# A residual of two gathered products: another way to the first adapter, the first x and the last y

## The reference

```python
def reference(x, itok_B_0_15, itok_B_3_7, L0_cond_weights, L1_cond_weight):
    W = L0_cond_weights[itok_B_0_15]                # (128, 64, 64): one of 16 per sample
    x = x + einsum('bct,bcd->bdt', x, W)            # x is (128, 64, 1024) float32
    w = L1_cond_weight[itok_B_3_7]                  # (128, 1024, 1024): one of 8 adapters
    x = x + einsum('bsi,boi->bso', x, w)
    return x
```

## Time and profile before

| | us |
|---|---|
| median of 3 runs | 836.09 |
| lowest, highest | 834.12, 836.31 |
| the profiled execution | 834.99 |
| its span in the profile | 833.2 |
| TensorE (PE) busy | 808.3 (97%) |
| VectorE (DVE) busy | 449.6 (54%) |
| ScalarE (ACT) busy | 280.6 (34%) |
| GpSimd (POOL) busy | 27.4 (3%) |
| DMA | 90.87 MB, mean 109 GB/s |

### The profile page before, as it was taken

One profiled execution on the slowest core, in us unless ns is written; L12 is line 12 of the kernel. 1 busy time (PEld: TensorE's weight loads), 2 busy tenths in 40 slices (PEclk: granted clock), 3 DMA queues, 4 the chain that ended last, 5 costly groups with the idle time before them and its releaser, 6 DMA issues.

```text
span 833.2 us, 17872 instructions
## 1 busy us (share of the span) xinstructions
PE 808.3 (97%) x3572; PEld 668.5 (80%) x3573; DVE 449.6 (54%) x466; ACT 280.6 (34%) x515; POOL 27.4 (3%) x61
## 2 busy tenths in 40 slices
...
DMA packets 74271, 90.87 MB, mean 109 GB/s; under 512 B 13844, under 2 KB 65044, under 8 KB 74260
## 3 DMA queue, kind: packets, MB, share of 16 engines
...
...
HBM read 57.15 MB, written 33.55 MB: 109 GB/s over the span
## 4 chain that ended last, share of the span: by engine, by line
PE 96%; DMA 1%; DVE 1%; issue 1%; SPq 1%; ACTq 0%; POOL 0%; POOLq 0%; ACT 0%; DVEq 0%
PE z_ps L431 14%; PE first_ps L431 14%; PE z_ps L430 14%; PE first_ps L430 14%; PE z_ps L433 14%; PE first_ps L433 13%; PE y_ps L445 4%; PE y_ps L446 4%; PE y_ps L444 4%; DMA w_nat<-in_L_cond_weight_dram 1%; SPq L343 0%; DMA slot_row<-table_i 0%; DMA ids_i<-in_itok_B_dram 0%; PE first_ps L411 0%; ACTq L192 0%
## 5 line engine op out<-in xcount | busy, mean ns | idle before, releaser
L430 PE MATMUL z_ps<-w_hi,xt_hi 128*128 (+1 forms) x528 | 205.5, 389 | 0.0
L431 PE MATMUL z_ps<-w_lo,xt_hi 128*128 (+1 forms) x528 | 205.4, 389 | 0.0
L430 PE MATMUL first_ps<-w_hi,xt_hi 128*128 x528 | 205.4, 389 | 0.0
L431 PE MATMUL first_ps<-w_lo,xt_hi 128*128 x528 | 205.4, 389 | 0.0
L433 PE MATMUL z_ps<-w_hi,xt_lo 128*128 (+1 forms) x512 | 199.2, 389 | 0.0
L433 PE MATMUL first_ps<-w_hi,xt_lo 128*128 x480 | 186.7, 389 | 0.0
L715 DVE STREAM_TRANSPOSE x_turned<-x_in 128x1024 f32<-128x1024 f32 x67 | 143.6, 2143 | 23.9 <-issue 19.5
L524 ACT ACTIVATE xt_hi<-x_turned 128x1024 fp32r<-128x1024 f32 x67 | 71.1, 1061 | 227.7 <-DVE x_turned L715 227.7
L724 DVE TENSOR_TENSOR xt_lo<-x_turned,xt_hi 128x1024 fp32r<-128x1024 f32 x62 | 76.1, 1228 | 77.8 <-ACT xt_hi L524 77.8
L430 PEld LDWEIGHTS z_ps<-w_hi,xt_hi 128*128 128x128 f32 x528 | 99.2, 188 | 20.9
L430 PEld LDWEIGHTS first_ps<-w_hi,xt_hi 128*128 128x128 f32 x528 | 99.1, 188 | 20.8
...
## 6 DMA issues: line engine op xcount, KB each, us to landing
x_in<-in_x_dram SPq DMA_DIRECT2D x544, 64.0 KB, 2.0
out_dram<-y ACTq DMA_DIRECT2D x128, 256.0 KB, 3.1
w_nat<-in_L_cond_weight_dram SPq DMA_DIRECT2D x128, 128.0 KB
...
x_turned<-in_L_cond_weights_dram SPq DMA_DIRECT2D x2, 256.0 KB, 3.9
ids_i<-in_itok_B_dram SPq DMA_DIRECT2D x2, 0.5 KB, 2.1
```

What stands on the lines that cost most here:

```text
L430: nc.tensor.matmul(to, xt_hi[h][:, t, :], whi, start=(t == 0), stop=False)
L431: mm = nc.tensor.matmul(to, xt_hi[h][:, t, :], wlo, start=False, stop=last and not pair)
```

## The change

The first adapter's number no longer comes from the groups: VectorE multiplies 8, 7, ... 1 by "used" and takes the largest (`first_row`). SP waits for that, loads chunks 0 to 5 at once, then x of slot 0 as plain rows in two transfers, its samples read straight from `table_i`, then chunks 6 and 7. TensorE turns x of slot 0 between chunks 3 and 4, through the same PSUM banks, and ACT and VectorE keep it from there. The table is moved by a DMA of ACT's queue, behind ACT's first chunk; GpSimd does chunks 0 to 3, the table's column, chunks 4 and 5, the group steps (on `is_group`, now made behind the table), chunks 6 and 7. The +1 on W goes from GpSimd to VectorE, between the one-hot matrices and the gathered values; the rest of W is made after the chunks instead of before them.

ACT's loop is now an odd and an even slot, and the last slot stands behind it, where y of the slot before is stored ahead of the second half of z. The last y is summed with the matmul on `z_lo` last, ACT writes its first half and VectorE its second, and SP and ACT store a sample each, in halves. The diff, declarations and unchanged arguments left out:

```diff
+        X0 = "x of slot 0"
+        TURN_ORDER = [0, 1, 2, 3, X0, 4, 5, 6, 7]
+        TURN_OF = {what: i for i, what in enumerate(TURN_ORDER)}
+        FOR_FIRST_HALF = 5
...
+        def store_last(eng, k, pairs_past):
+
+            s = 2 * pairs_past + 1
+            *samples, stores = look(eng, s, SAMPLE_A, SAMPLE_B, STORES)
+            rows = slice(k * C, (k + 1) * C)
+            to = out_rows[bass.ds(samples[k] * C, C), :]
+            with eng.If(stores > k):
+                eng.wait_ge(y_made, 4 * pairs_past + 3)
+                eng.dma_start(to[:, 0:HALF], y[1][rows, 0:HALF]).then_inc(last_stored, 16)
+                eng.wait_ge(last_half_made, 1)
+                eng.dma_start(to[:, HALF:T], y[1][rows, HALF:T]).then_inc(last_stored, 16)
+            with eng.Else():
+                eng.sem_inc(last_stored, 32)
...
+            for c in range(4):
+                add_1_to_first(c)
+            pool.wait_ge(table_moved, 16)
+            nc.gpsimd.tensor_copy(slot_row[:, 1:LOOKED_UP + 1, CHUNKS_BEFORE], slot_row[:, 0:LOOKED_UP, CHUNKS]
+                                  ).then_inc(table_ready, 1)
+
+            for c in range(4, 6):
+                add_1_to_first(c)
             pool.wait_ge(groups_made, 1)
...
-            for c in range(2, CHUNKS_PER_GROUP):
+            for c in range(6, CHUNKS_PER_GROUP):
                 add_1_to_first(c)
...
-            sp.wait_ge(groups_ready, 1)
-            first_ad = sp.value_load(group_row[0:1, 0:1], min_val=0, max_val=NAD - 1)
+            sp.wait_ge(first_known, 1)
+            first_ad = sp.value_load(first_row[0:1, 0:1], min_val=0, max_val=NAD - 1)
 
...
-                    sp.wait_ge(first_turned, NH * (c - OWN_PLACE) + NH)
+                    sp.wait_ge(first_turned, NH * TURN_OF[c - OWN_PLACE] + NH)
                 sp.dma_start(first_nat[c], adapter_rows[bass.ds((first_ad * CHUNKS_PER_GROUP + c) * P, P), :]
                              ).then_inc(first_loaded[c], 16)
 
-            for c in range(2):
+            for c in range(6):
                 load_first(c)
 
             sp.wait_ge(table_made, 1)
-            sp.dma_start(slot_row[:, 1:LOOKED_UP + 1, :], table_i[0:LOOKED_UP]).then_inc(table_moved, 16)
-            for c in range(2, 5):
+            _, first_samples = nc.values_load_multi_w_load_instructions(
+                table_i[0:1, SAMPLE_A:SAMPLE_B + 1], engines=[sp.engine], min_val=0, max_val=B - 1,
+                skip_runtime_bounds_check_because="the table is made on the chip, of clipped indices")
+            for k, sample in enumerate(first_samples):
+                sp.dma_start(x_in[0][k * C:(k + 1) * C, :], x_rows[bass.ds(sample * C, C), :]).then_inc(x0_loaded, 16)
+            for c in range(6, CHUNKS_PER_GROUP):
                 load_first(c)
...
             pairs_past = look_pairs_past(sp)
-            load_x(0, 0)
-            for c in range(5, CHUNKS_PER_GROUP):
-                load_first(c)
             load_x(1, 1)
 
-            sp.wait_ge(first_turned, NH * CHUNKS_PER_GROUP)
+            sp.wait_ge(groups_ready, 1)
+            sp.wait_ge(first_turned, NH * len(TURN_ORDER))
+            sp.sem_inc(x_loaded[0], PER_X)
...
+            store_last(sp, 0, pairs_past)
...
-                sp.wait_ge(y_stored[h], 32 * pairs_past + 32 + STORED_AHEAD)
+                sp.wait_ge(y_stored[h], 32 * pairs_past + (STORED_AHEAD if h else 32 + STORED_AHEAD))
                 sp.sem_inc(all_done, 1)
+            sp.wait_ge(last_stored, 64)
+            sp.sem_inc(all_done, 1)
...
+            def turn_first(i):
+                if TURN_ORDER[i] == X0:
+                    pe.wait_ge(x0_loaded, 32)
+                    nat = x_in[0][:]
+                else:
+                    pe.wait_ge(first_with_1, TURN_ORDER[i] + 1)
+                    nat = first_nat[TURN_ORDER[i]]
...
-                        pe.wait_ge(first_lo_made, NH * (c - TURNS) + n + 1)
+                    if i >= TURNS:
+                        pe.wait_ge(first_lo_made, NH * (i - TURNS) + n + 1)
...
             def first_half(pair):
-                pe.wait_ge(xt_lo_made, 1)
-                pe.wait_ge(first_lo_made, NH * TPB)
+                pe.wait_ge(first_lo_made, NH * FOR_FIRST_HALF)
                 sum_z(0, 0, 0, pair)
...
-                sum_y(2 * pairs_past + 1, pair)
+                s = 2 * pairs_past + 1
+                for k in range(2):
+                    pe.wait_ge(w0_placed[k], s + 1)
+                w0_slot, rows = (w0_parts, P) if pair else (w0_twice, C)
+                for n in range(NH):
+                    to = y_ps[n][0:rows]
+                    pe.wait_ge(z_hi_made, NH * s + n + 1)
+                    nc.tensor.matmul(to, w0_slot[:, 0], z_hi[:, n], start=True, stop=False)
+                    nc.tensor.matmul(to, w0_slot[:, 1], z_hi[:, n], start=False, stop=False)
+                    pe.wait_ge(z_lo_made, NH * s + n + 1)
+                    nc.tensor.matmul(to, w0_slot[:, 0], z_lo[:, n], start=False, stop=True).then_inc(y_summed, 1)
...
+                    tiles = slice(n * TPB, (n + 1) * TPB)
+                    to = xt_hi[0][:, tiles] if what == X0 else w_hi[:, 0, tiles, what * P:(what + 1) * P]
+                    act.wait_ge(first_turned, NH * i + n + 1)
...
                 place_w0_a(s)
+                if last_of_all:
+                    store_y(before, 1 - h)
                 keep_z_hi(s, h, 1)
-                store_y(before, 1 - h)
-
-            for c in range(4):
-                keep_first_hi(c)
-            keep_xt_hi(0, 0)
-            for c in range(4, CHUNKS_PER_GROUP):
-                keep_first_hi(c)
+                if not last_of_all:
+                    store_y(before, 1 - h)
+
+            keep_first_hi(0)
+            act.wait_ge(table_made, 1)
+            act.dma_start(slot_row[:, 1:LOOKED_UP + 1, :], table_i[0:LOOKED_UP]).then_inc(table_moved, 16)
+            for i in range(1, len(TURN_ORDER)):
+                keep_first_hi(i)
+            act.sem_inc(xt_hi_made, 1)
...
             pairs_past = look_pairs_past(act)
-            slot(0, 1, 0)
             with act.Fori(0, pairs_past) as i:
+                slot(i, 1, 2 * i)
                 slot(i + 1, 0, 2 * i + 1)
-                slot(i + 1, 1, 2 * i + 2)
+            slot(pairs_past, 1, 2 * pairs_past, last_of_all=True)
             act.wait_ge(y_stored[1], 32 * pairs_past + STORED_AHEAD)
-            make_y(2 * pairs_past + 1, 1)
-            store_y(2 * pairs_past + 1, 1)
+            act.wait_ge(y_summed, 4 * pairs_past + 3)
+            nc.scalar.activation(y[1][:, 0:HALF], y_ps[0][:], ACT.Copy).then_inc(y_made, 1)
+            store_last(act, 1, pairs_past)
...
+            nc.vector.tensor_scalar(countdown[:], col_i[0:1, 0:NAD], -1.0, float(NAD), ALU.mult, ALU.add)
             link(nc.vector.tensor_copy(col[:], col_i[:]))
...
             dve.wait_ge(counted, 1)
+            link(nc.vector.tensor_scalar(cnt[:, 1, :], counts_ps, 1.0, None, ALU.min))
+            link(nc.vector.tensor_tensor(countdown_used[:], countdown[:], cnt[0:1, 1, :], ALU.mult))
+            link(nc.vector.tensor_reduce(first_from_end[:], countdown_used[:], AX_X, ALU.max))
+            nc.vector.tensor_scalar(first_row[:], first_from_end[:], -1.0, float(NAD), ALU.mult, ALU.add
+                                    ).then_inc(first_known, 1)
             nc.vector.tensor_copy(looked[:, 0, :], ranks_ps)
-            nc.vector.tensor_scalar(cnt[:, 1, :], counts_ps, 1.0, None, ALU.min)
             link(nc.vector.tensor_scalar(pairs_i[:], counts_ps, 1.0, None, ALU.add))
             link(nc.vector.tensor_scalar(pairs_i[:], pairs_i[:], 1, None, ALU.logical_shift_right))
             link(nc.vector.tensor_copy(cnt[:, 0, :], pairs_i[:]))
...
+            dve.wait_ge(w0_loaded, 2 * 16)
+            nc.vector.tensor_tensor(w0_nat, w0_nat,
+                                    two_ident[:].rearrange("p (n d) -> p n d", n=1).to_broadcast([P, NCOND, C]),
+                                    ALU.add).then_inc(w0_with_1, 1)
...
+            nc.vector.tensor_tensor(is_group[:], looked[0:1, 2:3, :].to_broadcast([1, NAD, NAD]),
+                                    col[0:1, 0:NAD].rearrange("p (g u) -> p g u", u=1).to_broadcast([1, NAD, NAD]),
+                                    ALU.is_equal).then_inc(groups_made, 1)
...
+            def keep_x0_lo(i):
+
+                def keep(samples, to):
+                    for n in range(NH):
+                        at = (slice(None), slice(n * TPB, (n + 1) * TPB), samples)
+                        turned_x = first_banks[i % TURNS][n][:].rearrange("p (t m) -> p t m", t=TPB)[:, :, samples]
+                        dve.wait_ge(first_hi_made, NH * i + n + 1)
+                        nc.vector.tensor_tensor(to[at], turned_x, xt_hi[0][at].bitcast(F32),
+                                                ALU.subtract).then_inc(first_lo_made, 1)
+
+                stores, = look(dve, 0, STORES)
+                with dve.If(stores > 1):
```

(15 more changed lines are left out.)

58 lines of the change are left out of this document (22 added, 36 removed).

## The result

The changed kernel takes 830.22 us (median of 6 runs, 828.85 to 832.51), the kernel before 836.02 on the same chip (6 runs). The medians lie 5.8 us apart; the ratio, which takes all the runs in, is 0.9941 with a 95% interval of 0.9928 to 0.9954, which is a gain of 4.9 us (3.8 to 6.0) where 10 were forecast. 830.2 lies in the predicted range, at its upper end. The profiled execution of the changed kernel is the quickest of the six, 828.85, with a span of 827.1.

| us, in the profiled executions | before | after | won | forecast |
|---|---|---|---|---|
| up to the first long matmul | 32.53 | 28.10 | 4.4 | 7.2 |
| from there to the first y of the last slot | 792.2 | 793.0 | -0.8 | 0 |
| from there to the end of the span | 8.45 | 6.02 | 2.4 | 2.3 |

What follows compares the result with a forecast made beforehand. TensorE, busy 97% of the span, bounds the kernel, with 793 us left untouched. Span 833.2 - 7.2 (head) - 2.3 (end) = 823.7, giving 825.5 from the profiled execution or 826.6 from the median; forecast 826.0 us, range 822.5 to 830.5.

Steps and rivals of the forecast that it cites:

- First load: Start of the kernel: a shorter chain to the adapter's number lets the first load go at 8.3, 3.1 us earlier.
- x of slot 1 no wait: After the first long matmul: x of slot 1 ready at 33, wanted at 36.1, slack 3, so covered.
- the end: After the last slot's matmuls: earlier stores of y on two queues end the span at 830.9, 2.3 us earlier.
- The chunks: Head: loads land 1.4 us apart, chunk 7 at 23.6, so the first long matmul comes at 25.3, 7.2 earlier.
- four slow ones from 12.2 end at 19: TensorE's turns in the head: four at 0.21 us a transpose end at 19, when x is just there.
- rival (a): Head: loads land late, or the table at 21.5 holds chunks 4 to 7; matmul 27 to 28.5; 828.5; chance 0.15.
- The table: Head: `table_i` at 14.1, issued by ACT at 14.8, landed 17.8, taking 3 between bounds 2.3 and 6.7.
- "Nothing" in the middle: The long matmul stream: ACT's rotated loop has the same work per turn and costs nothing while TensorE covers it.
- rival (d): Middle: ACT's loop or late VectorE or SP leaves a gap each turn; 842.5 at 0.5 us; chance 0.03.
- no wait in 793 us: Middle of the kernel before: no TensorE wait over 793 us, used as evidence against gaps in each turn.
- Rival (b): Head: transposes stay at 1.2 GHz, matmul at 27.9, stream starts at half pace; 831; chance 0.07.
- (c): Start of the stream: x of slot 1 lands after 31.4, TensorE stops at 36.1; 3 us late gives 829; chance 0.05.

Runs made afterwards that it cites:

- a0: The changed kernel with each engine's group number and first chunk of a slot clamped at 0 by one register operation; 832.59 us, ratio 0.9959.
- e2: The changed kernel, clamped as a0, with 30 useless transposes ahead of TensorE's wait for x of slot 0; 830.89 us, ratio 0.9948.
- e4: a0 with x of slot 0 turned behind chunk 5 and GpSimd's chunks 4 and 5 ahead of the table's column; 830.12 us, ratio 0.9935.
- e6: a0 with x of slot 0 in eight transfers of 16 rows, the samples in turn; 829.71 us, ratio 0.9937.
- e7: a0 with x of slot 0 in two 64-row transfers from neighbouring samples in memory; 830.33 us, one run.
- e1: a0 with x of slot 0 in one transfer of 128 rows, so its second sample is another one; 827.84 us, ratio 0.9916.
- e8: a0 with the two samples of slot 0 on even and odd partitions, 64 rows each; 828.27 us, ratio 0.9915.
- e11: e4 and e8 together; 826.58 us, ratio 0.9909.
- e5: a0 with ACT's first odd slot ahead of its loop again, the last two slots behind it; 834.90 us, ratio 0.9997.
- e12: The changed kernel's head, clamped as a0, with ACT's loop and the end of the kernel before; 837.15 us, ratio 1.0029.
- e14: e11 with 32 semaphore increments that nobody waits for, ahead of ACT's first activation on W; 825.29 us, ratio 0.9890.

## Why the prediction was half right

**Right.** First load 8.27 (forecast 8.3); table made by 14.00 (14.1), ACT's issue 14.30 (14.8); issues of chunks 6 and 7 at 16.37 (16.3); x of slot 1 no wait; the end 2.4 (2.3), with a span that closes 3.1 behind the start of the last issue where I had added 3.3; no loss from a `z_lo` summed last.

**The step that failed** is the wait for x of slot 0, which the forecast did not have. It is in "The chunks": "4.7 MB are queued all along ... and so each of the next", at 1.4 us apiece, x's two transfers counted as any 256 KB of 4 KB rows, and with it, of TensorE's turns, "four slow ones from 12.2 end at 19, when x is just there". x was there at 22.36, 3.4 late, and in other executions still later (25.4 in a0). Three things are in it.

- The sum was wrong as it stood: at 1.4 apiece x is the sixth load behind the first, 11.4 + 6 x 1.4 = 19.8, not 19.
- The rows of x were slow. The chunks did flow at 395 to 404 GB/s. But each transfer of x wrote 64 neighbouring partitions, and while it did, 198 to 242 GB/s flowed in the six profiles that have neighbouring partitions (changed, a0, e2, e4, e6, e7), against 387 to 412 in e1, e8 and e11. No row of the kernel before had such a transfer in this direction; I had taken the row of a chunk, with 128 rows, as the nearest and given no bound for the other case. A sign was in the trace of before: from 22 to 23 us, with only pieces of x in transfer (1 KB packets, to a quarter of the partitions at a time), 223 GB/s flowed at a DMA share of 0.99. Packets of 1 KB may be slow for their own sake, so it does not settle the case, but it would have given the bound.
- x was late with quick rows too. In e1 and e8, which keep the forecast's order, x is turned at 21.28 and 21.63 after waits of 2.17 and 2.76, and the first long matmul is at 27.38 and 27.35. So of the 2.8 that the head fell short the slow rows account for 0.7 in the changed kernel's profile (28.10 to 27.38 and 27.35; 4.2 from a0's 31.61), and about 2 stay. They go only with the other order: 25.04 in e11. To put x ahead of chunks 4 and 5 in TensorE's queue was right only if x came at 19.

Two more things follow from the wait. TensorE's hole dropped its clock to 0.50 (21.7 to 25.2 in the changed kernel), worth 0.8 to 1.3 us by e2; it dropped in e1 and e8 as well. And the last chunk's landing no longer mattered: it was 25.3 for 23.6, yet its turn waited for its place in the queue till 27.29. The prediction had named the signs itself: no gap over 1 us in the turns (3.4), a first long matmul by 26.5 (28.10), no wait in the middle (0.5). Its rival (a) had the number, 27 to 28.5, but not the mechanism: neither three late loads nor the table's landing is what TensorE waited for.

**The table** was the second miss, a harmless one by itself: landed at 20.4 in place of 17.8, 6.1 behind its issue, beyond what I took (3), within what I had bounded (2.3 to 6.7). It is near rival (a)'s second half, "the table lands at 21.5". It is harmless only because x is later still: chunk 4 could not be added to before 20.7, so an x at 19 would have been followed by a wait for the table. It also takes 6.1 in e1 (14.21 to 20.33), where the rows of x are quick, so slow rows are not needed for that; with slow rows it takes up to 8.9 (a0). In e11 the order makes its lateness free: the column is made at 19.88, with no wait.

**"Nothing" in the middle** failed by 0.8 us in the profiled execution, and by up to 4.2 in relatives. That is rival (d) by its effect (VectorE, late relatively to TensorE, makes TensorE wait) but not by its mechanism: no gap in each turn (nearly all of it is two waits, near 145 and 151 us, around a short slot), no fault of the rotated loop (e5), but a first store that is slow to issue because ACT's instructions have shifted (e12, e14; one profile of each). I had read "no wait in 793 us" as slack; it showed only that the slack was not used up. How much was left was in no row that I looked at: about 1.3 us of lag (28.7 to 30.0), by the table above.

**Rival (b)** fell, and with it the rule of the Trainium skill's "TensorE: Matmul & The Clock Gate", "Part 4: PE-mode transpose", that the full clock does not engage for transposes: in the changed kernel the granted clock is 1.00 from 18.3 and again from 25.2, both in stretches with transposes alone, and eight of them then take 0.9. In e2 30 transposes of no use kept it there. By the Trainium skill's "DMA: Bandwidth & Descriptors", "Queues, rings and completion order", engines go in turn between the queue rows. The trace agrees as far as that: the table's 32-byte packets moved on ACT's row from 17.4 to 18.9, among SP's. But it was there only 6.1 behind its issue, so what I had drawn from the rule, that it would land near the low end of 2.3 to 6.7, failed.

The sum: of the 9.5 forecast in the span 6.1 came in the profiled execution, 2.8 lost in the head, 0.8 in the middle, 0.1 won at the end. The profiled execution was the quickest of six, so the typical gain is less (4.9 by the ratio). The landing of x moves: it is turned at 22.36 in this profile and at 23.4 to 25.4 in those of e6, e7, e2 and a0. That 830.2 still lies in the range is the range's width, which was meant for (a) and (c), and not this step foreseen.
